# A Fourier token mixer: another pixel layout, back transposition on VectorE, roots in pairs

## The chip, the cores and the metric

One NeuronCore of a Trainium2 chip runs the kernel in one launch. The metric is the device time of one execution in microseconds (us), as the median of three timed runs. One more execution was recorded by the hardware profiler; its trace gives every row shown here. The engines are TensorE (PE in the rows; PEld is its weight load), VectorE (DVE), ScalarE (ACT), GpSimd (POOL) and SyncE (SP), whose queue issues most of the loads. Weights, activations and sums are float32.

## What is computed

A tower of blocks on 64 images of 64 x 64 pixels with 3 values each. The first block, a Fourier token mixer, takes four fifths of the span; the change touches nothing else. Cut to it:

```
h = layer_norm(x @ fc0_w + fc0_b, ln0_g, ln0_b)        # 3 -> 32 channels
for i in range(4):
    x1 = spectral_conv(h, w1[i], w2[i])                # rfft2, 12 x 12 corner modes, irfft2
    x2 = einsum('bchw,oc->bohw', h, conv_w[i]) + conv_b[i]
    h = layer_norm(x1 + x2, ln_g[i], ln_b[i])          # over the 32 channels
    if i < 3: h = gelu(h)
h = gelu(h @ fc1_w + fc1_b); h = gelu(h @ fc2_w + fc2_b)
return (h @ fc3_w + fc3_b)[..., 0]                     # [64, 64, 64]
```

Attention, an expert FFN, a gated recurrence, a second expert FFN and layer norms follow on the result ("the token part", the last 632 us). They are left as they are.

## The kernel before

**Groups, phases, bodies.** The 64 images are worked in 16 groups of four. A phase makes one layer: *first* (fc0 with its layer norm, 16 bodies), three times *mid* (a spectral layer with gelu, 16 bodies each) and *last* (the fourth layer with fc1, fc2, fc3, 16 bodies); *into_last* is the body between mid and last. A body is one group's steps mixed with steps of the group before. In each layer 12 of the 16 bodies also carry three VectorE steps `cen.0` to `cen.2` that centre part of the next weights (L1574, L1576, L1578), and between bodies stand eight `mix` blocks in all, where the Fourier modes are multiplied by the weights.

**The table `ORDER`.** What each engine does in a body, and in what order, is written out by hand: one string per phase and engine. `acc.2` is step acc of quarter 2 of the group; a minus sign behind it means the group before. An engine runs its string strictly in order. A semaphore for each kind of step counts what is done; `PER` says how many counts a group makes in each phase.

**Steps of a group in mid.** A group has four quarters of 128 partitions x 1024 values. `i1` is the inverse transform along x (TensorE L1257, taken out of PSUM by VectorE's transposition L1592). `acc` sums the 1 x 1 convolution (L1285) and the inverse transform along y (L1293) in PSUM tile pA; ScalarE copies it to `w_sb` (L1425), squares it (`sq`, L1435), VectorE sums the squares (`red`, L1607). `rs` makes 1/sqrt of 32 variances a quarter in seven small VectorE instructions (`root`, L196 to L204). `scale` multiplies by that root on VectorE (L1621). `turn` transposes on TensorE (L1307) into pT, from which ScalarE's gelu goes to `h_new` (L1446). `back` transposes again on TensorE, eight 128 x 128 pieces into pS (L1315), and ScalarE copies them to `h_rows` (L1450) and issues the store of `h_new`. `f1` and `f2` are the forward transforms along y and x (TensorE L1329 and L1343, each taken out by VectorE, L1643 and L1649), and `pack` on ScalarE (L1459) sends the modes on.

In *first*, `xt` (L1242, L1420) transposes x and `acc` (L1275) is fc0. In *last* `back`, `f1` and `f2` give way to fc1 to fc3 (L1361, L1372, L1382).

**PSUM slots.** `RING` says in which PSUM tile a step's result lies: "d" is pD, "s" pS, "a" pA, "r" the halves of pT. d and s have one slot each: the next step of that ring may only be written by TensorE when the one before has been taken out.

**The start.** SP loads the constants and the first group's x (L967, two DMAs a group), waits for VectorE's memsets, and then loads fc0's weights sixteen times onto the diagonal of a 48 x 512 matrix (L973), its bias (L974) and the layer norm parameters. VectorE copies the bias sixteen times along a row (L1510) and centres fc0; then the first acc can start.

Of the kernel before, what the change touches and what calls it, by code (L numbers as in the profile page):

```python
# [51 lines left out]
def constants():  # L52
# [24 lines left out]
    for k in range(KX):  # L77
        c, t = np.cos(ang(k, y)), np.sin(ang(k, y))
# [41 lines left out]

PER = {
# [1564 lines left out]
```

## Time and profile before

| | |
|---|---|
| median of three runs | 3190.63 us (3189.6 to 3193.03) |
| the profiled execution | 3195.76 us |
| its span | 3194.0 us |
| TensorE busy | 2849.9 us (89%) |
| VectorE busy | 2238.3 us (70%) |
| ScalarE busy | 1881.4 us (59%) |
| first, 18.9 to 407 us | 388 us |
| three mid layers, 407 to 1908 us | 1501 us |
| last, 1908 to 2562 us | 654 us |
| token part, 2562 to 3194 us | 632 us |

Busy time counts instructions that compute; issuing a DMA or waiting on a semaphore is not busy. The span runs from the first to the last instruction of the profiled execution, and the run's own time holds 1.76 us more. A body's length is the distance between the same step in two bodies that follow each other.

### The profile page before, as it was taken

Reading aid. Unit: us, or ns where it says so; the run is one execution under the profiler, and the core shown is the slowest. Engines: PE = TensorE matmul, PEld = TensorE weight load, DVE = VectorE, ACT = ScalarE, POOL = GpSimd, SP = SyncE. Lnnn points to the kernel's source line nnn. Section 1 sums busy time; section 2 is a strip of 40 time slices with the busy share of each in tenths; the row PEclk is TensorE's granted clock in tenths of the full one; section 3 lists DMA queues with packets and bytes.
Section 4 is the critical chain, followed back from the end, with each engine's and each line's share of the span. In section 5 each row is a group of like instructions: output and inputs, shape, how many; then the busy total and the mean of one; then the engine's idle time right before and its main releaser. Section 6 shows DMA issues by size and latency. Waiting matters only on the chain.

```text
span 3194.0 us, 80965 instructions
## 1 busy us (share of the span) xinstructions
PE 2849.9 (89%) x31600; PEld 1808.1 (57%) x31600; DVE 2238.3 (70%) x4050; ACT 1881.4 (59%) x2175; POOL 61.8 (2%) x81
## 2 busy tenths in 40 slices
...
GB/s 98 133 99 86 88 171 182 208 167 167 131 170 157 215 169 162 128 191 148 226 165 160 134 145 96 66 58 59 60 60 60 30 1 1 1 1 0 1 1 14
DMA packets 98349, 335.89 MB, mean 105 GB/s; under 512 B 30185, under 2 KB 62217, under 8 KB 62345
## 3 DMA queue, kind: packets, MB, share of 16 engines
...
## 4 chain that ended last, share of the span: by engine, by line
PE 78%; DVE 11%; ACT 5%; issue 5%; DVEq 0%; SPq 0%; DMA 0%; ACTq 0%
PE pA L1285 15%; PE pA L1293 8%; PE pT L1372 7%; PE pT L1307 5%; PE pS L1315 5%; PE pD L1329 4%; PE pD L1361 4%; PE pD L1343 4%; PE pD L460 3%; PE pA L460 3%; PE pD L1257 3%; PE pA L1275 3%; PE pT L452 2%; PE pS L452 2%; DVE arena L1649 2%
## 5 line engine op out<-in xcount | busy, mean ns | idle before, releaser
L1285 PEld LDWEIGHTS pA<-conv_bd,h_in 128*128 128x128 f32 x4096 | 479.3, 192 | 107.3 <-issue 90.6
L1285 PE MATMUL pA<-conv_bd,h_in 128*128 128x128 f32 x4096 | 517.8, 280 | 6.9 <-DVE w_sb L1600 1.5
L1607 DVE TENSOR_REDUCE small<-arena 128x32 f32<-128x1056 f32 x320 | 397.5, 1242 | 170.3 <-ACT arena L1435 165.8
L1425 ACT COPY w_sb<-pA 128x1024 f32<-128x1024 f32 x256 | 259.7, 1014 | 392.3 <-PE pA L1293 343.3
L1621 DVE SCALAR_TENSOR_TENSOR w_sb<-w_sb,small 128x1024 f32<-128x1024 f32 x320 | 386.8, 1209 | 5.0
L1446 ACT ACTIVATE h_new<-pT,bet,gam 128x1024 f32<-128x1024 f32 x256 | 307.4, 1201 | 105.7 <-PE pT L1307 97.8
L1435 ACT ACTIVATE arena<-w_sb 128x1024 f32<-128x1024 f32 x320 | 339.4, 1061 | 14.7 <-DVE w_sb L1600 3.0
L1307 PEld LDWEIGHTS pT<-cst,w_sb 128*128 128x128 f32 x2048 | 225.4, 143 | 144.9 <-issue 124.4
L1307 PE MATMUL pT<-cst,w_sb 128*128 128x128 f32 x2048 | 283.2, 282 | 23.2 <-DVE w_sb L1621 23.1
L1450 ACT COPY h_rows<-pS 128x1024 f32<-128x1024 f32 x256 | 257.1, 1004 | 66.0 <-PE pS L1315 66.0
L1315 PEld LDWEIGHTS pS<-cst,h_new 128*128 128x128 f32 x2048 | 227.8, 142 | 112.3 <-issue 71.6
L1315 PE MATMUL pS<-cst,h_new 128*128 128x128 f32 x2048 | 274.6, 277 | 9.6 <-ACT h_new L1446 9.3
L1293 PE MATMUL pA<-arena,cst 64*64 64x512 f32 x2048 | 279.0, 615 | 0.0
L1372 PE MATMUL pT<-w_sb,arena 128*64 128x512 f32 x1024 | 251.7, 609 | 2.2 <-ACT w_sb L1479 1.7
L1343 PE MATMUL pD<-arena,cst 64*32 64x384 f32 (+1 forms) x4096 | 208.7, 494 | 11.7 <-DVE arena L1649 9.9
L1470 ACT ACTIVATE w_sb<-pD,arena 128x1024 f32<-128x1024 f32 x128 | 142.6, 1114 | 87.6 <-PE pD L1361 87.6
L1649 DVE STREAM_TRANSPOSE arena<-pD 128x768 f32<-128x768 f32 x128 | 125.5, 980 | 79.9 <-PE pD L1343 64.0
L1329 PE MATMUL pD<-h_rows,cst 64*32 64x512 f32 x2048 | 140.6, 603 | 37.3 <-DVE arena L1643 21.2
L1643 DVE STREAM_TRANSPOSE arena<-pD 128x1024 f32<-128x1024 f32 x128 | 159.3, 1244 | 10.7 <-PE pD L1329 6.7
L1372 PEld LDWEIGHTS pT<-w_sb,arena 128*64 128x64 f32 x1024 | 60.5, 136 | 171.9 <-issue 104.5
L1592 DVE STREAM_TRANSPOSE arena<-pD 128x1024 f32<-128x1024 f32 x96 | 119.9, 1249 | 50.6 <-PE pD L1257 49.9
L1361 PE MATMUL pD<-h_new,arena 32*128 32x512 f32 x512 | 144.4, 639 | 5.3 <-ACT w_sb L1470 3.6
...
## 6 DMA issues: line engine op xcount, KB each, us to landing
h_scratch<-h_new ACTq DMA_DIRECT2D x128, 1024.0 KB, 4.4
h_in<-h_scratch SPq DMA_DIRECT2D x128, 1024.0 KB, 5.2
...
y_in<-y_scratch SPq DMA_DIRECT2D x512, 36.0 KB
...
```

What stands on the lines that cost most here:

```text
L1285: pe.matmul(pA[:, c:c + 128], h_in[:, 1024 * n + c:1024 * n + c + 128], conv_bd[:], start=(j == 0), stop=False, skip_group_check=True)
L1293: mm = pe.matmul(pA[64 * b:64 * b + 64, 512 * t:512 * t + 512].rearrange("p (x o) -> p o x", o=C), const["idft_y"][rows, 64 * b:64 * b + 6 ...
L1307: mm = pe.transpose(pT[:, 128 * j:128 * j + 128], raw[n][:, 128 * j:128 * j + 128], ident)
L1315: mm = pe.transpose(bank[:, 128 * j:128 * j + 128], h_new[:, 1024 * n + 128 * j:1024 * n + 128 * j + 128], ident)
L1329: mm = pe.matmul(out[q:q + 32, b], const["dft_y"][rows, NQ * b:NQ * b + NQ], src[rows, t, 32 * xh:32 * xh + 32, 16 * ch:16 * ch + 16], sta ...
L1343: mm = pe.matmul(out.rearrange("p (q h c) -> p h c q", h=2, c=16), const["dft_x"][rows, 128 * part + 32 * j:128 * part + 32 * j + 32], TA[ ...
L1361: mm = pe.matmul((pD, pS)[k][:, 512 * b:512 * b + 512], fc1_w[rows, :], h_new[rows, 512 * u:512 * u + 512], start=True, stop=True)
L1372: mm = pe.matmul(bank[64 * j:64 * j + 64, :], fc2_w, G1[m % 4][:, 512 * j:512 * j + 512], start=True, stop=True)
L1435: act.activation(sq[n % 2][:, :, 0:C], raw[n].rearrange("p (x o) -> p x o", o=C), ACT.Square, scale=float(C) ** -0.5).then_inc(s["squared" ...
L1446: act.activation(h_new[:, 1024 * n:1024 * n + 1024], pT[:], ACT.Gelu if ph == "mid" else ACT.Identity, bias=bet[:, col], scale=gam[:, col] ...
L1607: dve.reduce_sum(var[n], sq[n % 2], axis=AX).then_inc(s["summed"], 1)
L1621: dve.scalar_tensor_tensor(out=z, in0=z, scalar=ROOT_SCALE, in1=r.broadcast_to([P, 32, C]), op0=ALU.mult, op1=ALU.mult).then_inc(s["normed ...
```

## The change

The pixel of an image is laid out in another way: one bit of x and the low bits of y lie on the partitions. The constants are permuted to fit (`x_fwd`, `x_inv`, `idft_y`). With this layout:

- `back` leaves TensorE and ScalarE: VectorE transposes `h_new` to `h_rows` in 32 x 32 blocks, one instruction of 128 x 1024 for a quarter (L1650). The store of `h_new` becomes a step `put` of its own on ScalarE.
- `rs` makes the roots of two quarters at once, on 128 x 64 values, in first and mid; in last it stays as it was. `scale`, the product with the root, stays on VectorE.
- `i1` (mid) and `f2` move to ring s, `f1` keeps ring d; `f2` waits for its own half of `f1` alone.
- `idft_y` in acc and fc3 run as twice as many matmuls of half the columns; fc0's acc works on 64 rows at a time; `fin` is two activations for one.
- x is loaded in 16 DMAs a group (runs of 24 values) after VectorE has cleared `h_in` and set a row of ones in it; the bias is part of the matrix, so fc0 takes 34 DMAs, and the copy of the bias is gone. `xt` is 8 matmuls of 64 columns.
- The strings of `ORDER` are new for first, mid and into_last.

```diff
+    x_inv = 32 * bit(y, 3, 1) + 16 * bit(y, 5, 1) + 8 * bit(y, 4, 1) + bit(y, 0, 3)
+    x_fwd = 32 * bit(y, 0, 1) + 16 * bit(y, 5, 1) + 8 * bit(y, 3, 1) + 2 * bit(y, 1, 2) + bit(y, 4, 1)
...
-    put("idft_y", iy.reshape(P, P))
+    put("idft_y", iy.reshape(P, 2, 2, C).transpose(0, 2, 1, 3).reshape(P, P))
...
+XLOADS = 16
...
-    "rooted":        (4, 0, 4, 4),
+    "rooted":        (2, 0, 2, 4),
...
-    "x_in":          (32, 0, 0, 0),
+    "x_in":          (XLOADS * 16, 0, 0, 0),
...
     "first": {
-        "PE": ("xt.0 turn.2- back.1- acc.0 back.2- turn.3- acc.1 back.3- acc.2 f1.0- turn.0 f1.1- acc.3 f2.0- back.0 "
-               "turn.1 f2.1-"),
...
-        "DVE": ("red.3- rs.3- scale.3- cen.0 cen.1 cen.2 red.0 rs.0 scale.0 red.1 f1.0- rs.1 f1.1- red.2 scale.1 "
-                "f2.0- rs.2 f2.1- scale.2"),
+        "PE": ("xt.0 turn.1- acc.0 turn.2- acc.1 turn.3- acc.2 f1.0- acc.3 f1.1- f2.0- f2.1- turn.0"),
+        "ACT": ("xt.0 gelu.1- acc.0 gelu.2- sq.0 acc.1 gelu.3- sq.1 put.0- put.1- acc.2 sq.2 acc.3 pack.0- sq.3 pack.1- gelu.0"),
+        "DVE": ("red.3- scale.1- rs.1- scale.2- cen.0 cen.1 back.0- cen.2 back.1- scale.3- back.2- red.0 back.3- red.1 f1.0- rs.0 scale.0 f1.1- f2.0- red.2 f2.1-"),
...
     "mid": {
-        "PE": ("i1.0 turn.2- back.1- acc.0 i1.1 turn.3- back.2- acc.1 back.3- acc.2 f1.1- turn.0 f1.0- acc.3 f2.0- "
-               "turn.1 f2.1- back.0"),
...
-        "DVE": ("red.3- i1.0 rs.3- scale.3- cen.0 cen.1 i1.1 red.0 rs.0 scale.0 red.1 rs.1 f1.1- scale.1 red.2 f1.0- "
-                "rs.2 f2.0- cen.2 scale.2 f2.1-"),
+        "PE": ("i1.0 turn.1- acc.0 i1.1 turn.2- acc.1 turn.3- acc.2 f1.0- acc.3 f1.1- f2.0- f2.1- turn.0"),
+        "ACT": ("gelu.1- acc.0 put.0- gelu.2- sq.0 acc.1 gelu.3- sq.1 acc.2 sq.2 acc.3 sq.3 pack.0- gelu.0 pack.1- put.1-"),
+        "DVE": ("red.3- i1.0 scale.1- rs.1- scale.2- cen.0 back.0- back.1- i1.1 cen.1 scale.3- back.2- red.0 cen.2 back.3- red.1 f1.0- red.2 rs.0 scale.0 f1.1- f2.0- f2.1-"),
...
-    "first": dict(xt="s", back="s", f1="d", f2="d"),
-    "mid": dict(i1="d", back="s", f1="d", f2="d"),
+    "first": dict(xt="s", f1="d", f2="s"),
+    "mid": dict(i1="s", f1="d", f2="s"),
...
-                for b in range(2):
-                    sp.dma_start(x_in[64 * b:64 * b + 64], src[g][b]).then_inc(s["x_loaded"], 16)
+                for e in range(2):
+                    for b in range(2):
+                        for t in range(2):
+                            for h in range(2):
+                                q = 64 * e + 32 * b
+                                sp.dma_start(x_in[q:q + 32, t, :, 24 * h:24 * h + 24], src[g][e, b, t][:, h]).then_inc(s["x_loaded"], 16)
...
+            sp.wait_ge(s["x_ready"], 1)
             load_x(0)
-            sp.wait_ge(s["fc0_chain"], 1)
-            for x in range(16):
-                sp.dma_start(fc0[3 * x:3 * x + 3, x, :], ins["L0_tok_fc0_w"]).then_inc(s["fc0_loaded"], 16)
...
+            sp.wait_ge(s["fc0_clear"], 1)
...
+            for t in range(2):
+                for h in range(2):
+                    for x in range(8):
+                        q = 64 * t + 24 * h + 3 * x
+                        sp.dma_start(fc0[q:q + 3, 2 * x + h, :], ins["L0_tok_fc0_w"]).then_inc(s["fc0_loaded"], 16)
+                sp.dma_start(fc0[64 * t + 48:64 * t + 49], fc0_bias).then_inc(s["fc0_loaded"], 16)
...
-                def back(n, g):
-
-                    pe.wait_ge(s["h_new_ok"], at("h_new", ph, L, g, n + 1))
-                    bank = bank_of("back", n, g)
-                    for j in range(8):
-                        mm = pe.transpose(bank[:, 128 * j:128 * j + 128], h_new[:, 1024 * n + 128 * j:1024 * n + 128 * j + 128], ident)
-                    send(mm, "back", n, g)
...
                 def f2(b, g):
 
+                    p.taken(pe, ("f1", b), g=g)
                     bank = bank_of("f2", b, g)
...
+            dve.memset(h_in[:, 0:512], 0.0).then_inc(s["fc0_chain"], 1)
+            dve.wait_ge(s["fc0_chain"], 1)
+            dve.memset(x_in[:, :, :, 48:49], 1.0).then_inc(s["x_ready"], 1)
+            dve.memset(T2[:, 1024:1536], 0.0).then_inc(s["fc0_clear"], 1)
+            dve.wait_ge(s["fc0_loaded"], 16 * 34)
...
-                    dve.wait_ge(s["summed"], at("summed", ph, L, g, 1 * h + 1))
+                    size = 1 if ph == "last" else 2
+                    dve.wait_ge(s["summed"], at("summed", ph, L, g, size * h + size))
...
+                def back(n, g):
+
+                    dve.wait_ge(s["h_new_ok"], at("h_new", ph, L, g, n + 1))
+                    dve.transpose(h_rows[:, 1024 * n:1024 * n + 1024], h_new[:, 1024 * n:1024 * n + 1024]).then_inc(s["h_rows_ok"], 1)
```

The order on VectorE at the end of a mid body, before. L1649 takes f2 out, L1578 is `cen.2`, L1621 is `scale.2`, L929 closes the loop, and L1607 is `red.3` at the head of the next body.

```order
L1649 STREAM_TRANSPOSE arena<-pD 128x768
L1571 ISA
L1578 SCALAR_TENSOR_TENSOR w_sb<-w_sb,cst,small 128x32x24
L1621 SCALAR_TENSOR_TENSOR w_sb<-w_sb,small 128x1024
L1647 REGISTER_ALU
L892 REGISTER_ALU
L1649 STREAM_TRANSPOSE arena<-pD 128x768
L929 REGISTER_ALU
L929 COMPARE_AND_BRANCH
L929 UNCONDITIONAL_BRANCH
L929 ISA
L1607 TENSOR_REDUCE small<-arena 128x32
```

The same place after the change. L1626 is `scale.0`, L1653 takes f1.1 out, L1660 f2, L1611 is `red.3`.

```order
L1626 SCALAR_TENSOR_TENSOR w_sb<-w_sb,small 128x1024
L890 REGISTER_ALU
L1653 STREAM_TRANSPOSE arena<-pD 128x1024
L890 REGISTER_ALU
L1660 STREAM_TRANSPOSE arena<-pS 128x768
L890 REGISTER_ALU
L1660 STREAM_TRANSPOSE arena<-pS 128x768
L927 REGISTER_ALU
L927 COMPARE_AND_BRANCH
L927 UNCONDITIONAL_BRANCH
L927 ISA
L1611 TENSOR_REDUCE small<-arena 128x32
```

The two f2 transpositions, which had `cen.2` and `scale.2` between them, now follow each other, behind the second f1; both read pS.

The order on TensorE from f2.0 to the end of a mid body, before. L1343 is f2 (16 matmuls each), L1307 `turn.1`, L1315 `back.0`.

```order
L1343 MATMUL pD<-arena,cst 32x32x12 x8
L1343 MATMUL pD<-arena,cst 32x32x11 x4
L1343 MATMUL pD<-arena,cst 32x32x12 x4
L1307 MATMUL pT<-cst,w_sb 128x128 x8
L1229 REGISTER_ALU
L1343 MATMUL pD<-arena,cst 32x32x12 x8
L1343 MATMUL pD<-arena,cst 32x32x11 x4
L1343 MATMUL pD<-arena,cst 32x32x12 x4
L1315 MATMUL pS<-cst,h_new 128x128 x8
```

The same place after. L1344 is f2, L1315 is now `turn.0`, L927 closes the loop.

```order
L1344 MATMUL pS<-arena,cst 32x32x12 x8
L1344 MATMUL pS<-arena,cst 32x32x11 x4
L1344 MATMUL pS<-arena,cst 32x32x12 x4
L897 REGISTER_ALU
L1236 REGISTER_ALU
L1344 MATMUL pS<-arena,cst 32x32x12 x8
L1344 MATMUL pS<-arena,cst 32x32x11 x4
L1344 MATMUL pS<-arena,cst 32x32x12 x4
L1315 MATMUL pT<-cst,w_sb 128x128 x8
L927 REGISTER_ALU
L927 COMPARE_AND_BRANCH
L927 UNCONDITIONAL_BRANCH
```

No `turn` stands between f2.0 and f2.1 any more, `back.0` is gone, and `turn.0` closes the body; f2 lies in pS.

SP's queue at the start, before: L967 loads x of the first group, L973 and L974 fc0's weights and bias, L978 and L979 a layer norm's gain.

```order
L967 DMA h_in<-in_x_dram 64x2x192 x2
L973 DMA arena<-in_L_tok_fc_w_dram 3x32 x16
L974 DMA arena<-in_L_tok_fc_b_dram 1x32
L978 DMA gam<-in_L_tok_ln_g_dram 32x1
L979 DMA gam<-in_L_tok_ln_g_dram 32x4x1
```

And after: L969 loads x, L980 and L981 fc0.

```order
L969 DMA h_in<-in_x_dram 32x4x24 x16
L980 DMA arena<-in_L_tok_fc_w_dram 3x32 x16
L981 DMA arena<-in_L_tok_fc_b_dram 1x16x32
L980 DMA arena<-in_L_tok_fc_w_dram 3x32 x16
L981 DMA arena<-in_L_tok_fc_b_dram 1x16x32
```

Sixteen loads of x stand ahead of fc0's, which come twice.

## Rows read from the trace of the kernel before

**Rows 1.** Part 1 of the page: busy us, share of the span, instructions.
```profile
PE 2849.9 (89%) x31600; PEld 1808.1 (57%) x31600; DVE 2238.3 (70%) x4050; ACT 1881.4 (59%) x2175; POOL 61.8 (2%) x81
```

**Rows 2.** Windows, a body of first, mid, last: us, PE, PEld, DVE, ACT, POOL busy, granted clock.
```profile
199.91:223.92 24.01, 21.05 (x186) 11.84 (x185) 21.27 (x43) 18.13 (x19) 0.00 (x0) 1.00 0.24 96
667.16:694.80 27.64, 26.57 (x322) 17.76 (x322) 23.79 (x45) 17.39 (x19) 0.00 (x0) 1.00 0.45 159
1974.00:2015.10 41.10, 41.08 (x322) 16.36 (x321) 28.21 (x48) 32.22 (x40) 0.00 (x0) 1.00 0.61 129
```

**Rows 3.** Timeline of VectorE in a mid body: start us, us.
```profile
667.16 1.25 DVE L1607 TENSOR_REDUCE small<-arena 128x32 f32<-128x1056 f32 x1 [1.06 <-ACT arena L1435]
...
677.38 0.98 DVE L1649 STREAM_TRANSPOSE arena<-pD 128x768 f32<-128x768 f32 x1 [1.00 <-PE pD L1343]
678.29 0.97 DVE L1578 SCALAR_TENSOR_TENSOR w_sb<-w_sb,cst,small 128x768 f32 x1
679.18 1.22 DVE L1621 SCALAR_TENSOR_TENSOR w_sb<-w_sb,small 128x1024 f32<-128x1024 f32 x1
680.32 0.98 DVE L1649 STREAM_TRANSPOSE arena<-pD 128x768 f32<-128x768 f32 x1
...
683.62 0.14 DVE L198 TENSOR_SCALAR small<-small 128x32 int32<-128x32 int32 x1
...
685.15 1.23 DVE L1621 SCALAR_TENSOR_TENSOR w_sb<-w_sb,small 128x1024 f32<-128x1024 f32 x1
```

**Rows 4.** Timeline of TensorE in the same body.
```profile
678.51 1.61 PE L1343 MATMUL pD<-arena,cst 64*32 64x384 f32 x32 [0.17 <-DVE arena L1649]
...
681.44 0.91 PE L1257 MATMUL pD<-y_in,cst 48*32 48x208 f32 x32 [0.30 <-DVE arena L1649]
```

**Rows 5.** Groups by line and form: busy us, mean ns of one.
```profile
L1632 DVE STREAM_TRANSPOSE h_new<-w_sb 128x1024 f32<-128x1024 f32 x64 | 79.3, 1240 | 1.1
...
L199 DVE TENSOR_TENSOR small<-small 128x32 f32<-128x32 f32 x320 | 61.5, 192 | 11.0
...
L684 DVE TENSOR_TENSOR w_sb<-pA,arena 128x512 f32<-128x512 f32 x44 | 30.4, 691 | 91.8 <-PE pA L460 91.8
```

**Rows 6.** Timeline of the start: SP's queue, VectorE, TensorE.
```profile
1.05 0.91 DVE L1499 MEMSET pD<- 128x1024 f32 x1 [1.05 <-PEq L1675]
1.22 1.39 SPq L967 DMA_DIRECT2D h_in<-in_x_dram  x2
...
5.80 5.06 SPq L973 DMA_DIRECT2D arena<-in_L_tok_fc_w_dram  x16
...
12.08 0.42 DVE L1510 COPY arena<-arena 1x512 f32<-1x512 f32 x1 [6.31 <-DMA arena<-in_L_tok_fc_b_dram]
...
14.05 3.75 PE L1275 MATMUL pA<-arena 128*128 128x512 f32 x4 [7.06 <-DVE arena L1514]
```

**Rows 7.** DMA issues: KB each, median us to landing; SP's issue times.
```profile
h_in<-in_x_dram SPq DMA_DIRECT2D x32, 96.0 KB, 2.5
...
w_sb<-in_L_tok_conv_w_dram SPq DMA_DIRECT2D x4, 16.0 KB, 6.7
...
L967 SPq DMA_DIRECT2D h_in<-in_x_dram x32: 598/607/736, 1.2 to 345.1; - x32
```

**Rows 8.** Busy time and granted clock around waits of TensorE.
```profile
923.20:925.80 2.60, 0.01 (x1) 0.00 (x0) 0.53 (x2) 1.34 (x2) 0.00 (x0) 1.00 0.01 3
926.10:929.40 3.30, 3.30 (x42) 2.68 (x27) 2.38 (x7) 0.00 (x0) 0.00 (x0) 0.50 0.02 5
60.60:66.60 6.00, 3.34 (x19) 2.33 (x20) 5.30 (x16) 3.72 (x5) 0.00 (x0) 1.00 0.11 46
481.20:485.70 4.50, 1.42 (x79) 1.23 (x80) 1.86 (x2) 0.80 (x1) 0.00 (x0) 1.00 0.02 4
485.70:488.90 3.20, 3.20 (x40) 2.56 (x41) 1.51 (x4) 0.00 (x0) 0.99 (x2) 0.52 0.74 173
```

More of the change, by code:

```diff
@@ L77, in constants @@
     for k in range(KX):
[L78 removed]
+        c, t = np.cos(ang(k, x_fwd)), np.sin(ang(k, x_fwd))
         for w, sign in enumerate((1, -1)):
@@ L1379, in fc3 @@
                     bank = bank_of("fc3", h, g)
-                    for part in range(2):
-                        for u in range(4):
-                            mm = pe.matmul(bank[32 * u:32 * u + 32, :], fc3_pad[:, part, :], G2[8 * h + 4 * part + u],
-                                           start=(part == 0), stop=(part == 1), skip_group_check=True)
+                    for n in range(2):
+                        for e in range(2):
+                            for t in range(2):
+                                for k in range(2):
+                                    q = 64 * t + 32 * k
+                                    rows = G2[8 * h + 4 * n + 2 * t + e].rearrange("p (x h y) -> p h x y", h=2, y=32)
+                                    mm = pe.matmul(bank[q:q + 32, 256 * e:256 * e + 256], fc3_pad[:, n, :], rows[:, k],
+                                                   start=(n == 0 and e == 0), stop=(n == 1), skip_group_check=True)
                     send(mm, "fc3", h, g)
-                return dict(xt=xt, i1=i1, acc=acc, turn=turn, back=back, f1=f1, f2=f2,
+                return dict(xt=xt, i1=i1, acc=acc, turn=turn, f1=f1, f2=f2,
                             fc1=fc1, fc2=fc2, fc3=fc3)
@@ L1486, in fin @@
                         act.wait_ge(s["y_stored"], 64 * 2 * LAYERS)
-                    out = tok[:, bass.ds(g * 128, 128)].rearrange("p (b h n x) -> p b h n x", b=2, h=2, n=2)
-                    src = G3_t.rearrange("p (x r) -> p r x", r=32)[:, 0:4, :].rearrange("p (b n) x -> p b n x", b=2)
-                    act.activation(out[:, :, h], src, ACT.Identity, bias=fc3_b).then_inc(s["fin_done"], 1)
-                return dict(xt=xt, acc=acc, sq=square, gelu=gelu, back=back, pack=pack, fc1=fc1, fc2=fc2, fc3=fc3, fin=fin)
+                    out = tok[:, bass.ds(g * 128, 128)].rearrange("p (b e n x) -> p b e n x", b=2, e=2, n=4)
+                    src = G3_t.rearrange("p (e x r) -> p e r x", e=2, r=32)
+                    for b in range(2):
+                        ins_ = act.activation(out[:, b, :, 2 * h:2 * h + 2], src[:, :, 2 * b:2 * b + 2, :], ACT.Identity, bias=fc3_b)
+                    ins_.then_inc(s["fin_done"], 1)
+                return dict(xt=xt, acc=acc, sq=square, gelu=gelu, put=put, pack=pack, fc1=fc1, fc2=fc2, fc3=fc3, fin=fin)
             phases(act, "ACT", mix, steps)
```

119 lines of the change are left out of this document (54 added, 65 removed), and 6 rows, old and new, of the table ORDER.

## The prediction

> **What bounds the kernel now.** The profiled execution took 3195.76 us around a span of 3194.0; the median of the three timed runs, 3190.63, lies 5.1 below it. I make the sum as a difference on the span and add it to the median. TensorE is busy for 89% of the span [rows 1], but that is a mean over stages, so I read one body (one group of four images) of each phase [rows 2]. A body of first lasts 24.01 us with TensorE busy for 21.05 and VectorE for 21.27: neither is full. A body of mid lasts 27.64 with TensorE busy for 26.57: TensorE binds. A body of last lasts 41.10 with TensorE busy for 41.08. The 48 mid bodies and 16 last ones are thus TensorE's; VectorE has room only where it waits. In a mid body [rows 3] it stands idle 1.06 ahead of the fourth sum (L1607 at 667.16) and 1.00 ahead of the first f2 transposition (677.38), and in smaller waits.
>
> **What the change takes from TensorE and gives to VectorE.** Eight transpositions a step on TensorE and a copy on ScalarE become one VectorE transposition of 128x1024, four a group. That shape takes 1240 ns from SBUF to SBUF [rows 5]; VectorE's instructions begin some 0.07 before the last has ended (677.38 to 678.29 is 0.91 for a duration of 0.98 [rows 3]), so I count 1.17, four times 4.68. Bounds: 1.05 to 1.24 each.
>
> Paired roots: one of 32 values runs from 683.62 to 685.15, 1.53 [rows 3], four a group are 6.12. Of 64 values there is no row. Lower bound: 1.53, all fixed cost. Upper: 3.06, all per element. From 192 ns at 32 values and 691 at 512 (same operation, rows 5) an element costs 1.04 ns; seven instructions by 32 elements add 0.23. I take 1.77, nearest the row of 192 ns, two a group 3.54. VectorE thus gets 4.68 - 2.58 = +2.1 us a body.
>
> **Mid, VectorE's list.** By the same way of counting, from start to next start [rows 3]: four sums at 1.15 (1.25 less the overlap, as L1607's row), four products at 1.13 (679.18 to 680.32), two f1 and two i1 transpositions at 1.17, two f2 at 0.90 (677.38 to 678.29), two roots 3.54, four back transpositions 4.68, and in 36 of 48 bodies the centring, 1.40 + 0.15 + 0.89 = 2.44 (678.29 to 679.18 is its third part). Together 4.60 + 4.52 + 2.34 + 2.34 + 1.80 + 3.54 + 4.68 + 2.44 = 26.26, under 27.64.
>
> But the list now ends with f1.1, f2.0, f2.1, next to each other, and f2 lies in ring s, which has one slot. TensorE can only write f2.1 when VectorE has taken f2.0 out. Before, that trip is a row: the transposition starts at 677.38 and takes 0.98, f2.1's matmuls start 0.15 later, at 678.51, and take 1.61 [rows 4]; f2.1 could be read at about 680.19, 2.81 after the first. Two instructions (centring and product, 2.03) stood between; now nothing does. So 2.81 - 0.90 = 1.91 of idle time, and about 0.15 ahead of f1. Queued behind f2.1 on VectorE are the fourth sum and i1.0, whose bank is freed by f2.1, then product 1, for which TensorE's turn.1 waits. A mid body with centring becomes 26.26 + 1.91 + 0.15 = 28.3, bound by VectorE, against 27.64: **+0.68, 36 times, 24.5**. Without centring VectorE would need 25.9, and the chain f2.1, i1.0, product 1, turn.1 gives about what there is now: 0.
>
> **First.** VectorE: 4.60 + 4.52 + 3.54 + 2.34 + 1.80 + 4.68 + centring 2.68 (its parts now follow at once, so each waits for the one before) = 24.16. Between f2.0 and f2.1 stands one sum (1.15), so 0.75 of the trip is left: 24.9 against 24.0 or a little less: **+1.0 in 12 bodies, 12**; the other four 0. TensorE has only some 14 us of work left in it.
>
> **Start.** Before, x comes with two loads, SP issues fc0's loads from 5.80, 16 in 5.06 (0.316 each), and the first acc starts at 14.05 [rows 6]. Now SP waits for VectorE's memsets (one of 128x1024 takes 0.91; the list ahead of x_ready ends near 4.8), then issues 16 loads of x at 0.607 [rows 7] = 9.7, and comes to fc0 at 14.5, 8.7 later; there are 34 rather than 17, +5.4; the bias copy of 0.42 goes. 8.7 + 5.37 - 0.42: **+13.6**, and nothing hides it, since every later step needs the first acc. In later groups SP's 9.7 is hidden: with 2.5 to 6.7 us to land [rows 7] it is 12 to 16 of a 24 us body.
>
> **Last.** The matmuls of idft_y and fc3 are twice as many at half the columns, 32 more a body. From 16 of some 376 columns in 1.61 and 16 of some 200 in 0.91 [rows 4] the part of a matmul that does not go with columns is about 7 ns: 0.2 a body, **+3** (0 to 8).
>
> **The clock.** Twice in these rows TensorE stood nearly still and then ran at the lower level: after 2.60 us with 0.01 busy the next 3.30 us had a granted clock of 0.50 (1.2 of 2.4 GHz); after 4.50 us with 1.42 busy, 0.52 for 3.2 us. But six microseconds that began with 2.6 idle stayed at 1.00 [rows 8]. So a gap of 2.6 is even odds, and a longer one falls. In 3.30 us at half clock 1.65 us of work is lost.
>
> In first after the change product 3 comes behind the centring and two back transpositions: from the end of product 2 VectorE needs 2.68 + 2.34 + 1.13 = 6.15, in which TensorE has turn.2 (0.9) and one acc (about 1.0). With what the waits between them take it stands still up to 4.0 us ahead of turn.3. I take a fall in each of the 12 bodies: 0.9 through turn.3, gelu and back.3, and 1.5 as f2.1's trip is run at half clock: **2.4 by 12, 29**. In mid, from f2.1's matmuls to turn.1 VectorE has f2.1, a sum, i1.0 and product 1, 0.90 + 1.15 + 1.17 + 1.13 = 4.35, and TensorE turn.0 and i1.0, 1.75: a gap of 2.6. Ahead of f2.1 it waits for the transpositions of f1.1 and f2.0, some 2.0. I take a fall in half of the 48 bodies; 1.65 less the 0.65 by which TensorE's chain (27.6) lies under VectorE's (28.3): 1.0 by 24, **24**.
>
> What the pages make of it: the Trainium skill, "TensorE: Matmul & The Clock Gate", section "HAM oscillation — how this bites in real kernels", says that bursts parted by waits are throttled again at each burst, and that the transition is paid every time, not once. By it all 48 mid bodies would have a fall. Of the gaps in rows 8 two agree and one does not; the case is (f) below. And the Trainium skill, "DMA: Bandwidth & Descriptors", Specifications, says that transfers under 512 B miss line rate; x now comes in runs of 96 bytes rather than 768. No row has such a load of x; the row of 6.7 us in rows 7 is used above as the bound without it.
>
> **Sum.** 13.6 + 12 + 24.5 + 3 + 29 + 24 = 106: 3300 on the span, **3297** on the median.
>
> **Rivals.** (a) The clock holds: 53, so **3244**. For it: the row of 60.60, and the mid bodies run at 1.00 throughout [rows 2]; against it: the gaps in first are longer than the one that fell. 0.16. (b) It falls in first only: 82, **3273**. 0.14. (c) It falls twice a mid body, or catches f2.1 there as well: the wait of 1.91 grows by 1.5 and turn.1 comes 0.9 late, 2.4 rather than 0.5 by 48: **3388**. For it: a late f2.1 lengthens the next gap, so that falls can feed themselves. 0.17. (d) Loads of x are late: if landing takes over 14 us rather than 2.5, xt.0 waits in 15 bodies; 5 us each gives **3370**. Against it: 6.7 us, the median of the loads with the smallest runs among the rows. 0.04. For it speaks also the page of the Trainium skill on DMA named above. (e) The other side: f2.1's wait is hidden. f2 now waits for its own f1 only and has a ring apart from f1's, so TensorE might have f2.1 done as VectorE comes to it; then a mid body is VectorE's 26.4, -1.23 by 36 = -44, and with 13.6 + 12 + 3 the sum is -16: **3175**, faster. It decides where the wait is under 0.43 us (a body of 26.84: 36 by -0.8 pays for the rest). Against it: one slot, and the trip in rows 3 and 4. 0.05.
>
> (f) A fall in every mid body, once: 24 more, **3321**. For it: both gaps of a body come every 28 us; against it: the row of 60.60. 0.13.
>
> **Chances.** The forecast has 0.31 with its own range 3280 to 3312, (a) to (f) 0.69. The range that leaves out no more than 2 in 10 runs from just under (a) to just over (c): 3238 to 3392; the bounds of the root (2 x 1.3 more at most, but only 0.5 less) and of the back transposition (4 x 0.12 less) move the middle by some 20 within it. Under 0.2%, 6 us, a measurement of this kernel tells nothing from no change. Faster 0.05 (case e), same 0.04 (between e and a), slower 0.91.
>
> **What would show it.** In the trace after: VectorE's back transpositions at 1.24; L199 at 225 ns; f2.1 starting 2.8 after f2.0 in mid, with about 1.9 of idle time between them put down to TensorE's f2; mid bodies of 28.3 to 29.5 in place of 27.64 and first bodies of some 27; the first acc near 27.6; stretches of a granted clock of 0.5 behind gaps ahead of turn.3 in first. I am wrong if f2.1 starts under 1.4 after f2.0, if mid bodies stay under 27.6, or if the clock stays at 1.00 throughout first.

## The result and the profile after

The changed kernel took 3384.27 us (median of four runs, 3383.55 to 3388.16) against 3190.11 for the kernel before: a ratio of **1.0613**, 95% interval 1.0596 to 1.063. It is slower by 6%. (Some executions of e8, of e11 and of the kernel before beside e5 to e8 and e11 were disturbed, at a lower clock and some 5% longer; they are left out of every time and ratio.) Page part 1 of the profile after, and from part 2 the clock granted to TensorE in 40 slices of the span (9 is 90% or more):

```profile
PE 2740.7 (81%) x32240; PEld 1788.9 (53%) x32240; DVE 2385.3 (71%) x3411; ACT 1637.0 (48%) x1951; POOL 61.8 (2%) x81
...
PEclk8888889888988988889898887999999997996897
```

TensorE is busy for 109 us less than in [rows 1], but the span is 3383.1 us rather than 3194.0, and its clock has 8s in the first two thirds. Where the 189 us lie is read from the starts of the first f2 transposition of a group in VectorE's timeline. Here is that of group 16, in first and in the third mid layer, before (L1649) and after (L1660):

```profile
435.79 0.98 DVE L1649 STREAM_TRANSPOSE arena<-pD 128x768 f32<-128x768 f32 x1 [1.03 <-PE pD L1343]
...
1885.31 0.98 DVE L1649 STREAM_TRANSPOSE arena<-pD 128x768 f32<-128x768 f32 x1 [3.32 <-PE pD L1343]
```

```profile
485.06 0.94 DVE L1660 STREAM_TRANSPOSE arena<-pS 128x768 f32<-128x768 f32 x1
...
2065.34 0.98 DVE L1660 STREAM_TRANSPOSE arena<-pS 128x768 f32<-128x768 f32 x1 [1.94 <-PE pS L1344]
```

| stretch | before | after | difference |
|---|---|---|---|
| start to group 1 of first | 50.44 | 65.36 | +14.9 |
| to group 16 of first | 385.35 | 419.70 | +34.4 |
| to group 16 of the third mid layer | 1449.52 | 1580.28 | +130.8 |
| to the end | 1308.69 | 1317.76 | +9.1 |

Bodies of first, mid and last by window, in the columns of [rows 2]:

```profile
200.59:227.74 27.15, 18.38 (x160) 8.35 (x160) 23.57 (x34) 13.68 (x15) 0.00 (x0) 0.81 0.25 85
713.83:744.49 30.66, 25.82 (x320) 17.98 (x320) 25.98 (x36) 13.65 (x14) 0.00 (x0) 0.89 0.41 147
2300.00:2341.20 41.20, 41.15 (x399) 18.65 (x391) 28.21 (x48) 32.60 (x43) 0.00 (x0) 1.00 0.18 58
```

A first body went from 24.01 to 27.15 and a mid body from 27.64 to 30.66. The windows of last were cut at 41.10 and 41.20; by the starts of VectorE's sums a body there went from 41.14 to 41.19. In the mid body TensorE's mean clock is 0.89, VectorE is busy for 25.98 of 30.66 us and TensorE for 25.82: nothing is full. VectorE's timeline at the end of that mid body, which answers to [rows 3]:

```profile
712.67 1.24 DVE L1653 STREAM_TRANSPOSE arena<-pD 128x1024 f32<-128x1024 f32 x1
713.83 0.94 DVE L1660 STREAM_TRANSPOSE arena<-pS 128x768 f32<-128x768 f32 x1
716.97 0.98 DVE L1660 STREAM_TRANSPOSE arena<-pS 128x768 f32<-128x768 f32 x1 [2.20 <-PE pS L1344]
717.88 1.21 DVE L1611 TENSOR_REDUCE small<-arena 128x32 f32<-128x1056 f32 x1
720.05 1.25 DVE L1596 STREAM_TRANSPOSE arena<-pS 128x1024 f32<-128x1024 f32 x1 [0.96 <-PE pS L1263]
721.23 1.18 DVE L1626 SCALAR_TENSOR_TENSOR w_sb<-w_sb,small 128x1024 f32<-128x1024 f32 x1
```

The list reads f1.1, f2.0, and then 2.20 us of nothing until TensorE's f2.1 is there: 716.97 is 3.14 after 713.83. Then comes the sum, another 0.96 of waiting for i1.0, and product 1. TensorE over the same time, to be held against [rows 4]:

```profile
714.92 2.01 PE L1344 MATMUL pS<-arena,cst 64*32 64x384 f32 x32 [1.98 <-DVE arena L1660]
716.87 1.97 PE L1315 MATMUL pT<-cst,w_sb 128*128 128x128 f32 x8
718.76 1.16 PE L1263 MATMUL pS<-y_in,cst 48*32 48x208 f32 x32
722.54 1.80 PE L1315 MATMUL pT<-cst,w_sb 128*128 128x128 f32 x8 [2.62 <-DVE w_sb L1626]
724.13 2.93 PE L1292 MATMUL pA<-conv_bd,h_in 128*128 128x128 f32 x16
```

It stood still for 1.98 us ahead of f2.1, whose matmuls took 2.01 (1.61 in [rows 4]), and for 2.62 ahead of turn.1, which took 1.80 (1.09 where the clock is 1.00, as at 570.39 below). The granted clock, which answers to [rows 8], around these two gaps of the mid body, and around the gap of a first body:

```profile
713.00:714.90 1.90, 0.00 (x0) 0.01 (x1) 1.77 (x2) 0.00 (x0) 0.00 (x0) 1.00 0.93 384
716.00:719.00 3.00, 3.00 (x32) 1.79 (x24) 2.03 (x2) 0.00 (x0) 0.00 (x0) 0.50 0.00 0
719.90:722.50 2.60, 0.02 (x7) 0.00 (x0) 2.45 (x3) 0.73 (x2) 0.00 (x0) 1.00 0.86 353
723.00:726.00 3.00, 3.00 (x16) 3.00 (x15) 2.83 (x7) 1.21 (x1) 0.00 (x0) 0.50 0.00 0
212.00:215.60 3.60, 0.00 (x0) 0.00 (x0) 3.60 (x5) 1.91 (x3) 0.00 (x0) 0.80 0.16 17
215.70:224.00 8.30, 7.46 (x32) 2.78 (x32) 6.01 (x7) 4.11 (x4) 0.00 (x0) 0.50 0.61 253
```

After the first gap (713.00, 0.00 us busy) the clock falls to the lower level, 1.2 GHz, by 716.00; it comes back, and after the second gap (719.90) it falls again. In first the clock falls within the gap and stays low for the 8.30 us behind it.

The clock doesn't fall in every mid body. Of the 36 that lie away from the ends of a layer, 31 have two falls (30.4 to 30.7 us), two have one, and three have none: these take 28.3 to 28.4. One of the three by window, and its two gaps on TensorE:

```profile
563.01:591.39 28.38, 22.53 (x320) 15.64 (x320) 25.76 (x36) 13.64 (x14) 0.00 (x0) 1.00 0.49 174
```

```profile
564.10 1.61 PE L1344 MATMUL pS<-arena,cst 64*32 64x384 f32 x32 [2.00 <-DVE arena L1660]
...
570.39 1.09 PE L1315 MATMUL pT<-cst,w_sb 128*128 128x128 f32 x8 [2.58 <-DVE w_sb L1626]
```

The gaps are as long as in the other body, 2.00 and 2.58 for 1.98 and 2.62. So two falls cost 2.3 us a body, and the length of the gaps alone doesn't decide whether they come.

TensorE's timeline behind the gap in first:

```profile
215.65 1.97 PE L1315 MATMUL pT<-cst,w_sb 128*128 128x128 f32 x8 [3.92 <-DVE w_sb L1626]
217.54 2.08 PE L1282 MATMUL pA<-arena 64*128 64x512 f32 x4
220.46 1.96 PE L1329 MATMUL pD<-h_rows,cst 64*32 64x512 f32 x16 [0.84 <-DVE h_rows L1650]
```

turn.3 waited 3.92 for product 3 and took 1.97; acc.2 and f1.0 behind it ran at half clock too. Finally the two prices that had no row before, and the start, which answers to [rows 6]:

```profile
L1650 DVE STREAM_TRANSPOSE h_rows<-h_new 128x1024 f32<-128x1024 f32 x256 | 312.0, 1233 | 53.9 <-ACT h_new L1448 53.9
...
L199 DVE TENSOR_TENSOR small<-small 128x64 f32<-128x64 f32 x128 | 28.8, 225 | 4.4
```

```profile
4.77 7.46 SPq L969 DMA_DIRECT2D h_in<-in_x_dram  x16
...
12.27 5.04 SPq L980 DMA_DIRECT2D arena<-in_L_tok_fc_w_dram  x16
...
26.59 2.08 PE L1282 MATMUL pA<-arena 64*128 64x512 f32 x4 [10.63 <-DVE arena L1518]
```

Two more places take time that the bodies above don't show. The first is the last body of each mid layer: 27.5, 27.5 and 28.9 us before, 35.9, 38.6 and 35.1 after, 25.8 more in all. SP loads the first group of the next layer only when group 15 has been stored to the end. In the new ScalarE string of mid that store, `put.1-`, comes last. Here are the store's issue on ScalarE, the load's on SP, and the acc on TensorE that waits for it:

```profile
977.27 0.35 ACTq L1456 DMA_DIRECT2D h_scratch<-h_new  x1
...
981.71 1.13 SPq L1002 DMA_DIRECT2D h_in<-h_scratch  x2
...
986.67 3.78 PE L1292 MATMUL pA<-conv_bd,h_in 128*128 128x128 f32 x16 [5.43 <-DMA h_in<-h_scratch]
```

The same acc waits 6.23 and 4.09 in the other two layers, and not at all in the kernel before, where the store is issued 11.2 ahead of that body's first f2 transposition; here it comes 4.4 behind it. The second place is one VectorE instruction in into_last. It takes 0.18 us in the median (0.80 at most in the kernel before) and took 7.38 here, and TensorE waited 7.37 for what comes behind it:

```profile
2090.23 7.38 DVE L198 TENSOR_SCALAR small<-small 128x32 int32<-128x32 int32 x1 [0.25 <-DVE small L1611]
```

### The profile page after: what moved, and what is told of

It is laid out like the page before. It is cut to its first block, busy times and chain, and to the rows that moved or that the text cites. A ratio compares the mean times of both kernels' runs of the same rounds, so it can differ in the third digit from the quotient of the medians.

```text
span 3383.1 us, 81821 instructions
## 1 busy us (share of the span) xinstructions
PE 2740.7 (81%) x32240; PEld 1788.9 (53%) x32240; DVE 2385.3 (71%) x3411; ACT 1637.0 (48%) x1951; POOL 61.8 (2%) x81
## 4 chain that ended last, share of the span: by engine, by line
PE 64%; DVE 17%; issue 13%; ACT 3%; SPq 1%; DMA 1%; DVEq 1%; ACTq 0%
PE pA L1292 13%; PE pT L1373 7%; PE pT L1315 7%; PE pA L1302 6%; PE pD L1362 4%; PE pS L1344 4%; PE pD L458 3%; PE pA L458 3%; PE pS L1263 3%; DVE w_sb L1626 3%; PE pD L1329 2%; DVE arena L1660 2%; PE pT L450 2%; PE pS L450 2%; PE pT L1387 2%
## 5 line engine op out<-in xcount | busy, mean ns | idle before, releaser
L1315 PE MATMUL pT<-cst,w_sb 128*128 128x128 f32 x2048 | 360.9, 333 | 200.3 <-DVE w_sb L1626 198.4
L1315 PEld LDWEIGHTS pT<-cst,w_sb 128*128 128x128 f32 x2048 | 285.0, 170 | 343.1 <-issue 217.0
L1611 DVE TENSOR_REDUCE small<-arena 128x32 f32<-128x1056 f32 x320 | 390.1, 1219 | 99.6 <-ACT arena L1437 97.2
L1626 DVE SCALAR_TENSOR_TENSOR w_sb<-w_sb,small 128x1024 f32<-128x1024 f32 x320 | 386.6, 1208 | 5.0
L1650 DVE STREAM_TRANSPOSE h_rows<-h_new 128x1024 f32<-128x1024 f32 x256 | 312.0, 1233 | 53.9 <-ACT h_new L1448 53.9
L1344 PE MATMUL pS<-arena,cst 64*32 64x384 f32 (+1 forms) x4096 | 223.8, 524 | 127.6 <-DVE arena L1660 126.3
L1302 PE MATMUL pA<-arena,cst 64*64 64x256 f32 x4096 | 282.2, 391 | 0.0
L1344 PEld LDWEIGHTS pS<-arena,cst 64*32 64x32 f32 x4096 | 87.1, 108 | 247.5 <-issue 223.0
L1660 DVE STREAM_TRANSPOSE arena<-pS 128x768 f32<-128x768 f32 x128 | 123.1, 962 | 120.5 <-PE pS L1344 120.5
L1653 DVE STREAM_TRANSPOSE arena<-pD 128x1024 f32<-128x1024 f32 x128 | 159.5, 1246 | 40.7 <-PE pD L1329 40.6
L1596 DVE STREAM_TRANSPOSE arena<-pS 128x1024 f32<-128x1024 f32 x96 | 119.7, 1247 | 85.0 <-PE pS L1263 83.2
L1329 PE MATMUL pD<-h_rows,cst 64*32 64x512 f32 x2048 | 150.8, 647 | 23.6 <-DVE h_rows L1650 19.6
L1302 PEld LDWEIGHTS pA<-arena,cst 64*64 64x64 f32 x4096 | 132.4, 133 | 64.5 <-issue 2.9
```

Source lines behind the costliest of these rows:

```text
L1302: mm = pe.matmul(out[:, h], const["idft_y"][rows, 64 * h:64 * h + 64], T2_v[rows, xh, :, x:x + 8], start=False, stop=True, skip_group_chec ...
L1315: mm = pe.transpose(pT[:, 128 * j:128 * j + 128], raw[n][:, 128 * j:128 * j + 128], ident)
L1344: mm = pe.matmul(out.rearrange("p (q c) -> p c q", c=C), const["dft_x"][rows, 128 * part + 32 * j:128 * part + 32 * j + 32], TA[rows, b, : ...
L1611: dve.reduce_sum(var[n], sq[n % 2], axis=AX).then_inc(s["summed"], 1)
L1626: dve.scalar_tensor_tensor(out=z, in0=z, scalar=ROOT_SCALE, in1=r.broadcast_to([P, 32, C]), op0=ALU.mult, op1=ALU.mult).then_inc(s["normed ...
L1650: dve.transpose(h_rows[:, 1024 * n:1024 * n + 1024], h_new[:, 1024 * n:1024 * n + 1024]).then_inc(s["h_rows_ok"], 1)
```

## The experiments

Each edit is against the changed kernel, and stands here cut to its core. Where only one execution was timed, the kernel before ran beside it on the same chip.

**e1, filler in both gaps.**

```diff
 def turn(n, g):
+    if n >= 1 or not first_group(g):
+        pe.wait_ge(s["h_new_ok"], at("h_new", ph, L, g, n))
+    for j in range({"mid": 16, "first": 24}[ph] if n == {"mid": 1, "first": 3}[ph] else 0):
+        pe.transpose(pT[:, 128 * (j % 8):128 * (j % 8) + 128], ident, ident)
     pe.wait_ge(s["normed"], at("normed", ph, L, g, n + 1))
...
 def f2(b, g):
     p.taken(pe, ("f1", b), g=g)
+    if b == 1 and ph != "last":
+        pe.wait_ge(s["h_new_ok"], at("h_new", ph, L, g, 4))
+        for j in range(12):
+            pe.transpose(pT[:, 128 * (j % 8):128 * (j % 8) + 128], ident, ident)
```

> The changed kernel with useless transpositions of the identity on TensorE in its two gaps: 16 (mid) or 24 (first) ahead of turn.1 or turn.3, 12 ahead of f2.1, all written to pT, which the real turn overwrites. VectorE's and ScalarE's work stays as it is. Theory (the gaps let the clock fall twice in a mid body and once in a first body, and the falls cost 2.4 us each body): mid bodies 28.0 to 28.4 instead of 30.65, first bodies 24.8 to 25.3 instead of 27.1, granted clock 1.00 in both, about 3245 us (3235 to 3265): more work, shorter time. Rival (VectorE's added load of 2.1 us a body is the cost, and what TensorE does meanwhile doesn't matter): bodies and time as in the changed kernel, 3384, or longer.

Measured: 3303.34 (before 3192.93), mid bodies 28.77 to 28.90, first bodies about 25.9. Useless work made the kernel 81 us faster, so the rival falls; but the size was missed by 58 us. The filler began only when f1.1 had been taken out, and so held up f2.1 itself. e10 moves it.

**e10, the same filler earlier.** The loop of 12 stands ahead of `p.taken(pe, ("f1", b), g=g)`, and 12 rather than 16 stand ahead of turn.1.

> Both fillers as in e1, but the 12 ahead of f2.1 issued right behind f2.0, before TensorE waits for f1.1 to be taken out, and 12 rather than 16 ahead of turn.1, so that f2.1 isn't held up by them. Theory (e1's bodies of 28.8 held 0.5 us of the filler's own delay): mid bodies 28.0 to 28.4, the sum worked out for VectorE's list with the clock held (28.3), clock 1.00, 3275 us (3260 to 3290). Rival (28.8 is what VectorE's list needs): 3303 again.

Measured: 3270.88 (before 3186.97). A mid body by window, and in VectorE's timeline its two f2 transpositions:

```profile
715.85:744.11 28.26, 25.52 (x346) 18.23 (x345) 25.64 (x37) 13.64 (x14) 0.00 (x0) 1.00 0.45 160
```

```profile
715.85 0.94 DVE L1666 STREAM_TRANSPOSE arena<-pS 128x768 f32<-128x768 f32 x1
718.60 0.98 DVE L1666 STREAM_TRANSPOSE arena<-pS 128x768 f32<-128x768 f32 x1 [1.82 <-PE pS L1350]
```

The mid bodies away from the ends of a layer run at a clock of 1.00 and take 28.26 to 28.39, some 28.5: the sum for VectorE's list. The trip from f2.0 to f2.1 is 2.75 with a wait of 1.82. What is left against 30.66, 2.3 us a body, is the price of the falls, as in the three bodies of the changed kernel that have none.

**e9, the filler ahead of turn alone** (e1 without its part in f2).

> The filler of e1 ahead of turn.1 (mid) and turn.3 (first) alone; the gap of 2.0 us ahead of f2.1 stays, and f2.1 starts as early as in the changed kernel. Theory A (in mid neither gap makes the clock fall by itself, the two together do, as e3 suggests, where the gap of 2.7 alone did not): clock 1.00 in mid, mid bodies 28.0 to 28.5, first 25.0 to 25.8, 3270 us (3255 to 3290). Theory B (each gap of 2 us or more makes a fall by itself): a fall behind the gap ahead of f2.1 in each mid body, 29.0 to 29.8, 3320 us (3300 to 3345).

Measured: 3300.37 (before 3186.97). Neither theory: the clock falls in 17 of the 36 mid bodies away from the ends of a layer. Here is f2.1 in three bodies that follow each other, in VectorE's timeline:

```profile
696.62 0.98 DVE L1662 STREAM_TRANSPOSE arena<-pS 128x768 f32<-128x768 f32 x1 [1.82 <-PE pS L1346]
...
725.53 0.98 DVE L1662 STREAM_TRANSPOSE arena<-pS 128x768 f32<-128x768 f32 x1 [2.35 <-PE pS L1346]
...
754.57 0.98 DVE L1662 STREAM_TRANSPOSE arena<-pS 128x768 f32<-128x768 f32 x1 [1.82 <-PE pS L1346]
```

The wait is 1.82 where the clock held and 2.35 where it fell; these bodies last 28.3 and 29.6. So the gap of 2.0 ahead of f2.1 makes a fall by itself in some bodies and not in others, and one fall costs 1.3 us.

**e2, half of the back transposition.** Half of h_rows stays zero, so the Fourier part is computed from half the data.

```diff
-dve.transpose(h_rows[:, 1024 * n:1024 * n + 1024], h_new[:, 1024 * n:1024 * n + 1024])
+dve.transpose(h_rows[:, 1024 * n:1024 * n + 512], h_new[:, 1024 * n:1024 * n + 512])
...
+dve.memset(h_rows[:], 0.0)      # once, in the wait for fc0's weights
```

> The changed kernel with VectorE's back transposition at half its columns (128x512 for 128x1024), so that half of h_rows is left at zero and the Fourier part of each layer is computed from half the data; all else as it is. It takes some 2.3 us a body off VectorE. Theory (in mid the list's end, f1.1 f2.0 f2.1 i1.0 product 1, and the clock's falls set the body, not VectorE's load): mid bodies stay at 30.6 within 0.2; first bodies, where the two back transpositions lie in the gap ahead of turn.3, 24.0 to 25.5 instead of 27.1; about 3345 us (3330 to 3365). Rival (VectorE's load): 2.3 less in all 64 bodies, 3237.

Measured: 3348.10 (before 3192.93). A mid body by window:

```profile
717.70:748.37 30.67, 25.82 (x320) 18.07 (x320) 24.03 (x37) 13.65 (x14) 0.00 (x0) 0.89 0.41 144
```

VectorE is busy for 2 us less (24.03) and the body is as long as ever; TensorE's clock is 0.89. As long as the clock falls, VectorE's load isn't what a mid body pays for. In the five mid bodies of e2 where the clock held, the 2 us are worth 0.6: 27.7 rather than 28.3. In first, where back transpositions lie in the gap ahead of turn.3, bodies came down to 23.7 to 25.9.

**e3, two slots for f2.**

```diff
-    "mid": dict(i1="s", f1="d", f2="s"),
+    "mid": dict(i1="s", f1="d", f2="s", f2_1="d"),   # and the same in "first"
```

> The changed kernel with f2.1 in ring d (pD) rather than ring s, so that f2.0 and f2.1 have a slot each; the order of the instructions on every engine stays as it is. Theory (one slot makes VectorE wait 2.2 us for f2.1 and TensorE stand still 2.0 ahead of it, and both late steps feed the clock's falls): the wait ahead of f2.1 falls under 1.0, mid bodies 27.2 to 28.5, first 24.5 to 25.5, about 3190 to 3235 us. Rival (VectorE's load): the same instructions, 3384 less at most the wait itself, 1.3 by 64 = 83, 3300.

Measured: 3239.16 (before 3192.93), 145 us less with the same instructions in the same order. A mid body by window, the gap ahead of turn.1 and what follows it, and f2.1 in TensorE's timeline:

```profile
708.68:735.96 27.28, 22.52 (x320) 15.59 (x320) 25.55 (x36) 13.64 (x14) 0.00 (x0) 1.00 0.46 164
712.40:715.00 2.60, 0.00 (x0) 0.00 (x0) 2.60 (x4) 0.93 (x2) 0.00 (x0) 1.00 0.79 325
715.10:720.00 4.90, 4.90 (x74) 3.92 (x75) 4.69 (x9) 2.15 (x2) 0.00 (x0) 1.00 0.08 32
```

```profile
708.90 1.61 PE L1344 MATMUL pD<-arena,cst 64*32 64x384 f32 x32 [1.29 <-DVE arena L1653]
```

The mid body is 27.28, under the 27.64 of the kernel before. VectorE's wait ahead of f2.1 is 0.95, and the gap of 2.6 ahead of turn.1 is still there, but the clock holds, here and in 27 of the 36 mid bodies away from the ends of a layer: the same gap that is mostly followed by a fall in the changed kernel mostly isn't here, where TensorE stood still for 1.29 rather than 1.98 before it. First bodies stayed at 25 to 26.4, longer than expected, as the gap ahead of turn.3 still makes the clock fall (0.86 on average from 200 to 330 us), and the last bodies of the mid layers at 34 to 35; the total is just over its range.

**e4, another order, same instructions.** Two of its strings (scale.1 also leaves the late steps of into_last):

```diff
 mid, DVE
-cen.0 back.0- back.1- i1.1 cen.1 scale.3- back.2- red.0 cen.2 back.3- red.1 f1.0- red.2 rs.0 scale.0 f1.1- f2.0- f2.1-
+cen.0 back.0- back.1- i1.1 cen.1 scale.3- back.2- red.0 cen.2 back.3- red.1 f1.0- rs.0 scale.0 f1.1- f2.0- scale.1 red.2 f2.1-
 mid, PE
-acc.3 f1.1- f2.0- f2.1- turn.0
+acc.3 f1.1- f2.0- turn.0 f2.1-
 first, DVE
-red.3- scale.1- rs.1- scale.2- cen.0 cen.1 back.0- cen.2 back.1- scale.3- back.2- red.0 ...
+red.3- rs.1- scale.2- scale.3- cen.0 cen.1 back.0- cen.2 back.1- back.2- red.0 ...
```

> The changed kernel with another order and the same instructions: on VectorE product 0 and product 1 and the third sum around f2 (f2.0, product 1, sum 2, f2.1), so that product 1 no longer waits behind i1.0; in first product 3 right behind product 2, ahead of centring and back transpositions; on TensorE turn.0 between f2.0 and f2.1. Theory (the order of the list makes the waits, the waits make the clock fall): mid bodies 26.2 to 26.8, under the 27.64 of the kernel before, first 24.2 to 25.5, clock near 1.00 in mid, about 3150 us (3130 to 3185), faster than before. Rival (VectorE's load of 26.3 plus what every order has in waits): not under 27.6 a mid body, 3200 or more.

Measured: 3184.68 (before 3192.93). A mid body, and in a first body a gap and what follows it:

```profile
691.70:718.25 26.55, 22.46 (x321) 15.62 (x322) 25.67 (x35) 13.65 (x14) 0.00 (x0) 1.00 0.48 171
205.30:208.60 3.30, 0.00 (x0) 0.00 (x0) 3.30 (x4) 2.20 (x3) 0.00 (x0) 0.98 0.98 401
209.00:215.00 6.00, 5.63 (x40) 1.23 (x48) 4.59 (x11) 1.15 (x2) 0.00 (x0) 0.50 0.18 74
```

Most mid bodies take 26.55 to 26.7, 1 us under the kernel before. In first product 3 no longer makes TensorE wait, but the gap moved: it now lies ahead of f1.0, which waits for the four back transpositions, and the clock falls behind it. First bodies are 25.5 to 25.7, at the upper end or just over it, the last bodies of the mid layers are 34 to 37, and the total is at the upper end too: 8 us under the kernel before, less than that kernel's own executions differ by, so "faster" isn't shown. The rival falls.

**e5, the start.** fc0's matrix is cleared first, SP issues its loads at once, and ScalarE's queue issues the first x.

> The changed kernel with another start only: VectorE clears fc0's matrix and x first, SP begins fc0's 34 loads at once, and the 16 loads of the first group's x are issued on ScalarE's queue at the same time. Theory (the start costs what stands in SP's queue ahead of fc0's loads): the first acc at about 16.5 us instead of 26.6, 3374 us (3371 to 3377). Rival (the start is hidden behind later waits): 3384.

Measured: 3378.87 (before 3186.07). The first acc came at 15.81. The first f2 came at 52.54 rather than 65.36, 12.8 earlier, and 12.5 of it were still there at group 16 of first, so the start's cost is real. But the mid layers took 6.0 us longer than in the changed kernel (1586.2 for 1580.3), the last part 0.5, and only 5.4 are left in the total. Why the mid layers took longer, one execution of each doesn't tell.

**e6, roots one by one** (two of 32 where there was one of 64).

> The changed kernel with the roots made one by one, two of 32 values in a row at each place where it makes one of 64; the order stays. VectorE gets 2 x (3.06 - 1.75) = 2.6 us a body. Theory (VectorE's list is in the chain that sets a body in first and partly in mid, and a pair costs little more than a single): first bodies +1.9 to +2.6, mid +0.5 to +1.5, 3435 us (3410 to 3475). Rival (a pair costs as much as two singles, or VectorE has room for it): 3384 within 6.

Measured: 3538.65 (before 3186.07). Far more than expected: 154 us over the changed kernel. The two f2 transpositions of a mid body:

```profile
708.70 0.94 DVE L1664 STREAM_TRANSPOSE arena<-pS 128x768 f32<-128x768 f32 x1
712.67 0.98 DVE L1664 STREAM_TRANSPOSE arena<-pS 128x768 f32<-128x768 f32 x1 [3.03 <-PE pS L1344]
```

With the roots longer TensorE stands still for 3.62 rather than 1.98 us ahead of f2.1; its clock is at the lower level when f2.1 begins (0.50 from 709.80 to 712.50), f2.1 takes 2.81, and the trip from f2.0 is 3.97 (3.14 in the changed kernel). Most mid bodies are 32.4 to 33.7, first ones 29 to 30.6: about 2 and 3 more, where 0.5 to 1.5 and 1.9 to 2.6 were expected. The rival falls; the theory has the sign, and left out that with a gap of 3.62 the clock may be low before f2.1 begins.

**e7, e8 and e11, a version made from this.** The start of e5 and an order in which work stands in each of the trips; e8 has two slots for f2 in addition. VectorE's strings in e8:

```diff
+first: red.3- back.0- rs.1- scale.2- back.1- cen.0 scale.3- red.0 cen.1 back.2- back.3- cen.2 red.1 f1.0- rs.0 scale.0 f1.1- red.2 f2.0- f2.1- scale.1
+mid:   red.3- i1.0 rs.1- scale.2- cen.0 scale.3- i1.1 back.0- red.0 cen.1 back.1- back.2- back.3- cen.2 red.1 f1.0- rs.0 red.2 scale.0 f1.1- f2.0- scale.1 f2.1-
```

> The changed kernel with the start of e5 and a third order on all three engines: product 3 right behind product 2, the centring's three steps apart, product 1 and a sum between f2.0 and f2.1, in first acc.3 and turn.0 and in mid acc.3 between f2.0 and f2.1 on TensorE, pack.0 ahead of acc.3 on ScalarE. The work is the same. Theory (order, waits, clock): mid bodies 26.1 with centring, first 23.9, clock at 1.00 through both, about 3130 us (3112 to 3152), faster than before by 1.2 to 2.4%. Rival (VectorE's added work costs what it saves on TensorE): 3175 or more.

> As e7, with f2.1 in ring d, so that f2 has two slots, and the order fitted to that. Theory: with an order that puts work into the trip the second slot is worth nothing more: 3130 us, within 10 of e7. Rival (the slot is a cost of its own in any order): 15 us or more under e7.

> The kernel of e8 once more, since two of its four executions were disturbed. Theory: 3113 to 3120 us in undisturbed executions, 0.974 to 0.980 of the kernel before. Rival (e8's gain was one chip's): over 0.985.

Measured: e7 0.9948 of the kernel before (interval 0.9924 to 0.9973), 3168.75, where 1.2 to 2.4% less were expected; e8 0.9775 (0.9747 to 0.9803), two executions of 3113 and 3117; e11, the same kernel as e8, 0.9763 (0.9745 to 0.9781). A stretch of first and a mid body of e8:

```profile
171.50:196.00 24.50, 14.93 (x162) 7.57 (x160) 23.91 (x35) 14.39 (x17) 0.00 (x0) 1.00 0.30 99
704.37:730.37 26.00, 23.19 (x321) 15.65 (x320) 25.41 (x37) 13.78 (x14) 0.00 (x0) 1.00 0.52 181
```

Both run at a clock of 1.00, but in 8 of the first 13 bodies of first it still falls once (in 3 of them in e11); the mid body takes 26.00 us. e7, whose clock still falls in first and whose mid bodies are 26.7, was expected at 3130. e8 is 54 us faster, but the slot isn't all that differs. e8 also stores earlier: its ScalarE string in mid has `put.1-` ahead of `sq.2`, where e7 has it last. In e7's trace the acc at the end of a mid layer waits 8.9 to 10.0 us for its load, in e8 and e11 it doesn't, and these three bodies take 33 us less. So what the second slot itself is worth isn't shown, and the theory that a good order makes it worthless is left open.

## Why the forecast came out as it did

Direction and range held: slower, and 3384 lies within 3238 to 3392. The likeliest case, 3297, was not what happened: 194 us more, for 106. Nearest is rival (c), worked out at 3388, to which I had given 0.17. Its mechanism, two falls a body, is what the trace shows, but that its number came so close is partly luck: it holds 115 us for the falls in mid, where e10 makes them 91, and nothing for the ends of the mid layers.

- **VectorE's list and the one slot: right.** "28.3, bound by VectorE" is 28.26 to 28.39 in e10, where the clock is held up; the idle time in the trip, 1.91, is 1.82 there. For the 24.5 of this term, all mid bodies but the last of each layer take 19.6 more in e10 than in the kernel before.
- **The prices without a row: right.** L1650 takes 1233 ns; L199 on 64 values 225 ns, 33 more than on 32, as the 1.04 ns an element of the estimate has it. Pairing is a gain, as e6 shows.
- **The falls in mid: the term that was mis-sized.** "I take a fall in half of the 48 bodies; 1.0 by 24, 24." The mechanism was right. But the clock falls twice in 31 of the 36 bodies away from the ends of a layer, which costs 2.3 us a body (30.66 less 28.38; one fall costs 1.3 in e9). In e10 the mid layers take 1489.7 us rather than 1580.3: the falls cost 91 us there, for 24. The reason that rival (c) gives, that a late f2.1 lengthens the next gap, isn't borne out: the second gap is 2.62 behind a fall and 2.58 in the body without one. The two gaps do hang together: with the first at 1.29 (e3) the second mostly brings no fall, and with the second filled (e9) the first brings one in half of the bodies. Whether it is the sum of the gaps, the time between them or something else isn't shown.
- **The ends of the mid layers: a term at nothing.** The last body of each layer takes 25.8 us more in all, 20.6 in e10. The change put a store last in ScalarE's string, and the sum has no term for who waits for it. Falls, list and layer ends make up the mid layers: 90.6 + 19.6 + 20.6 is the 130.8 of the table, for 24 + 24.5.
- **First: near, partly by luck.** 34.4 for 12 + 29. Bodies of 27.15 were forecast as "some 27"; the gap ahead of turn.3 is 3.92, said to be "up to 4.0". But in e10, where the clock holds in most of its bodies, first still takes 22 more than before. If the filler itself costs nothing there, waits and list are 22, for 12, and the falls 12, for 29.
- **The start: right.** The first acc at 26.59 is 12.5 late, for 13.6: SP issued a load of x in 0.47, not 0.61. The first f2 is 14.9 late; the second group's x was late as well (rival d, below).
- **Last: too low.** 9.1 for 3. A body is 0.05 longer, 0.8 for 16. Most of the rest is the wait of 7.37 in into_last for the VectorE instruction of 7.38. TensorE's timeline has a wait of 7.36 or 7.37 at that place in e2, e4, e5, e6 and e7 too, and none of that length there in the kernel before or the other runs; what makes the instruction so long no run tells.
- **Rival (e), f2.1's wait hidden: refuted** by the 2.20 in VectorE's timeline. **Rival (d), late loads of x: true once.** TensorE's timeline has xt waiting for x at the start and, for 4.44 us, at 44.83 in the second group, whose loads stood behind fc0's and the layer norm's in SP's queue; from the third group on it doesn't wait. A load lands in 1.7 us (median of 256).
